# Two-layer attention and expert kernel on one core: group buffers, scatter order, unused norm products, and one tile step moved

## What is computed

```python
x = x + L0_attn(xn) + L0_ffn(xn);  xn = layernorm(x)
x = x + L1_attn(xn) + L1_ffn(xn)
# L0_attn: q, k(2), v(2) = xn + xn @ W.T + b; feature map silu(.)+0.5 on q and k, divided by
#          the norm of each head (16 heads of 8); state = prod over the 2 kinds of k^T v;
#          out = q state; layernorm with gain and bias; @ Wo.T + bo
# L0_ffn:  8 experts of 128x128, the best one for each token, y * its softmax weight
# L1_attn: 16 heads, window of 32, plus 8 latent heads over 64 pooled rows, gates, @ w_out
# L1_ffn:  8 experts 128 -> 512 (relu) -> 128, the best two for each token, weighted sum
```

## Time and profile before

| | |
|---|---|
| three runs | 658.37, 658.41, 660.02 us |
| profiled execution | 655.52 us; its span 653.8 us |
| busy in the span | PE 510.1 (78%), DVE 410.6 (63%), ACT 280.7 (43%), POOL 272.4 us (42%) |
| chain that ended last | PE 50%, DVE 20%, no visible wait ("issue") 10%, POOL 9%, ACT 6%, DMA 3% |
| mean granted TensorE clock | 0.859 of full speed |

### The profile page before, as it was taken

How to read it: one execution, slowest core, us unless ns; L and a number is a source line. 1 busy time by engine, 2 the same in 40 slices (tenths; PEclk the granted TensorE clock), 3 DMA queues, 4 the chain that set the end, 5 groups by cost and what they waited for, 6 DMA issues and landing times.

```text
span 653.8 us, 19837 instructions
## 1 busy us (share of the span) xinstructions
PE 510.1 (78%) x7216; PEld 419.8 (64%) x7216; DVE 410.6 (63%) x1113; ACT 280.7 (43%) x714; POOL 272.4 (42%) x321
## 2 busy tenths in 40 slices
PE   6929947696642786389778889998999898988765
PEld 3926737585630573267556878896889687977544
DVE  6678867575536946995968364646465554565572
ACT  1315742443320115153536666565656564654320
POOL 6064573455758000277676223141314140414830
PEclk8658967987885757598999999999999998999775
DMA  9999113434402600011112634242415240510991
GB/s 246 220 249 190 37 50 93 135 113 140 140 18 69 188 1 2 17 55 53 47 56 61 218 110 151 69 162 86 155 57 183 77 158 35 180 63 14 135 209 48
DMA packets 80237, 70.12 MB, mean 107 GB/s; under 512 B 7604, under 2 KB 65779, under 8 KB 80142
## 3 DMA queue, kind: packets, MB, share of 16 engines
q1 hardware_dynamic: 62528, 50.87, 28.1%
q0 software_dynamic: 15072, 16.90, 11.3%
q10 hardware_dynamic: 2542, 1.08, 0.7%
HBM read 22.73 MB, written 23.22 MB: 70 GB/s over the span
## 4 chain that ended last, share of the span: by engine, by line
PE 50%; DVE 20%; issue 10%; POOL 9%; ACT 6%; DMA 3%; DVEq 0%; ACTq 0%; POOLq 0%; SPq 0%
PE psum L1816 8%; PE psum L1805 8%; POOL sorted L694 6%; PE psum L1304 3%; PE psum L559 2%; PE psum L852 2%; PE psum L1238 2%; DVE st_all L498 2%; PE psum L974 2%; PE psum L1349 2%; DVE x_all L490 2%; ACT arena L1440 2%; PE psum L1327 2%; PE psum L1359 2%; PE psum L953 2%
## 5 line engine op out<-in xcount | busy, mean ns | idle before, releaser
L1878 POOL DMA_INDIRECT ydram<-xnT_all,f_id x71 | 69.3, 976 | 177.1 <-DVE f_id L1851 124.2
L694 POOL DMA_INDIRECT sorted<-xr_all,slot x96 | 95.7, 997 | 44.6 <-issue 26.5
L1836 ACT ACTIVATE xr_all<-psum,b1T 128x128 f32<-128x128 f32 x284 | 81.1, 369 | 28.9 <-PE psum L1805 27.8
L1816 PE MATMUL psum<-w,xr_all 128*128 x568 | 76.6, 278 | 1.6 <-DVE xnT_all L1859 1.4
L1805 PE MATMUL psum<-xr_all 128*128 128x128 f32 x568 | 77.1, 279 | 0.0
L1859 DVE TENSOR_TENSOR xnT_all<-psum,b_bc 128x128 f32<-128x128 f32 x71 | 20.7, 292 | 88.2 <-PE psum L1816 84.6
L1805 PEld LDWEIGHTS psum<-xr_all 128*128 128x128 f32 x568 | 69.8, 194 | 4.0 <-issue 3.4
L1816 PEld LDWEIGHTS psum<-w,xr_all 128*128 128x128 f32 x568 | 69.2, 192 | 3.2 <-issue 2.6
L1507 ACT ACTIVATE arena<-arena 128x512 f32<-128x512 f32 x32 | 20.1, 630 | 67.0 <-DVE arena L1594 65.5
L837 POOL DMA_INDIRECT ydram<-arena,g_id x40 | 40.6, 1015 | 11.2 <-issue 10.7
L1327 PE MATMUL psum<-arena 128*128 128x128 f32 (+3 forms) x64 | 22.5, 471 | 17.6 <-DVE arena L1574 10.4
(11 more groups left out here) (284 smaller groups left out, 1166.6 us busy)
## 6 DMA issues: line engine op xcount, KB each, us to landing
xr_all<-arena SPq DMA_DIRECT2D x71, 256.0 KB
arena<-mix SPq DMA_DIRECT2D x40, 128.0 KB, 2.0
sorted<-pre_row SPq DMA_DIRECT2D x1, 4680.0 KB, 29.4
xnT_all<-sorted SPq DMA_DIRECT2D x18, 260.0 KB, 3.2
x_all<-ydram POOLq DMA_DIRECT2D x16, 256.0 KB, 9.7
sorted<-pre_row SPq DMA_DIRECT2D x1, 2600.0 KB, 21.1
arena<-sorted SPq DMA_DIRECT2D x10, 260.0 KB, 3.0
x_all<-in_L_attn_x_dram SPq DMA_DIRECT2D x8, 256.0 KB, 6.0
```

The costliest lines, as they stand in the source:

```text
L694: g.indirect_dma_start(out=dst, out_offset=bass.IndirectOffsetOnAxis(ap=slot[:, choice, t:t + 1], axis=0), in_=xr_all[:, t, :], in_offset= ...
L1816: mm = pe.matmul(psum[:, 3, 0:C], f_hT[n % 3][:, j * P:(j + 1) * P], w2[:, bass.ds(e * FC + j, 1), :].rearrange("p a f -> p (a f)"), start ...
L1836: ins = act.activation(f_hT[n % 3][:, j * P:(j + 1) * P], psum[:, 1 + rr % 2, j * P:(j + 1) * P], ACT.Relu, bias=b1T[:, bass.ds(e * FC + j ...
L1878: g.indirect_dma_start(out=ydram, out_offset=bass.IndirectOffsetOnAxis(ap=f_id[rr][:, 1:2], axis=0), in_=f_y[rr % 4], in_offset=None, boun ...
```

## The change

- `norm_pe`, both layers: in front of each batch's wait for its rows, TensorE makes 5 products of 128x256 bf16 whose result nobody reads (PSUM bank 2, columns 256 to 511).
- `biases_pool`: the 10 instructions run first on the 384 columns of the query and key biases, with no wait for VectorE, and later, after VectorE's fifth step, on the 128 columns of the output bias. TensorE waits for the second set only before `states`, VectorE before its features.
- Layer 0, TensorE: queries and keys of batch 0 come before `routing_pe`. ScalarE's two tanh of batch 0 stand alone, in the same place of its order as before.
- `states`: `g_y` and `g_id` have four buffers, `g_y` in the space of the transposed rows (`xnT`) of batches 0 to 3; VectorE waits for the scatters of group n-4 instead of n-2. POOL scatters `mid` in front of the addition.
- `mixed` on ScalarE: one of the three tile steps stands between the copy of the queries and that of the keys.

```diff
+        def unused_halves(pe, n):
+            for _ in range(n):
+                pe.matmul(psum[:, 2, 256:512], onesb[:, 0:P], onesb[:, 0:256], start=True, stop=True,
+                          skip_group_check=True)
...
+        def bias_parts(g, lo, hi, done):
+            q = slice(lo, hi)
+            g.tensor_copy(bparts[:, 0, q], brow[:, q]).then_inc(s_bp, 1)
...
         def biases_pool(g):
             g.wait_ge(s_w, 16 * N_W)
+            bias_parts(g, 0, 3 * C, 0)
             g.wait_ge(s_setv, N_SETV)
...
+            bias_parts(g, 3 * C, 4 * C, N_BP)
...
+        def two_deep(eng, stage, begun=False):
+            if not begun:
+                stage(eng, None, (0, 0))
...
                     k = b + B * layer
+                    unused_halves(pe, 5)
                     pe.wait_ge(s_xn, k + 1)
...
-        g_y = [view(4 * C).rearrange("p (j c) -> p j c", j=4) for _ in range(2)]
+        GY, GID = 4, 4
+        g_y = [xnT(b).rearrange("p (j c) -> p j c", j=4) for b in range(GY)]
+        g_id = [view(4, dt=I32) for _ in range(GID)]
...
+        def group_scattered(eng, n):
+            if n >= 0:
+                eng.wait_ge(g_sc[n % GID], (n // GID + 1) * 64)
...
         def group_numbers(v, n):
-            if n >= 2:
-                v.wait_ge(g_sc[r], n // 2 * 64)
+            group_scattered(v, n - GID)
...
         def group_results(v, n):
-            if n >= 2:
-                v.wait_ge(g_sc[r], n // 2 * 64)
+            group_scattered(v, n - GY)
...
+        def feat_tanh(act, cur):
...
         def feat_act(act, prev, cur):
-            if cur:
+            if cur and prev:
+                feat_tanh(act, cur)
...
         def state_pool(g, three, two, one, mid, behind):
+            group_pool(g, mid)
             if three:
...
-            group_pool(g, mid)
             group_pool(g, behind)
...
         def y0_loads(sp):
-            for r in range(2):
-                sp.wait_ge(g_sc[r], 64 * (NGR // 2))
+            for n in range(NGR - GID, NGR):
+                group_scattered(sp, n)
...
                 queries(b + 1)
+                tiles.go(1)
                 keys(b + 1)
                 pooled_rows(b + 1)
-                tiles.go(3)
+                tiles.go(2)
...
             routing_act(act, 0)
+            feat_tanh(act, (0, 0))
             two_deep(act, feat_act)
...
             routing_dve(v, 0)
+            v.wait_ge(s_bp, 2 * N_BP)
             two_deep(v, feat_dve)
...
-            routing_pe(pe, 0)
             pe.wait_ge(s_bp, N_BP)
             pe.wait_ge(s_lgu, 1)
-            two_deep(pe, feat_pe)
+            feat_pe(pe, None, (0, 0))
+            routing_pe(pe, 0)
+            two_deep(pe, feat_pe, True)
             pe.wait_ge(s_w2, 16 * N_W2)
+            pe.wait_ge(s_bp, 2 * N_BP)
```

More of the change, by code:

```diff
@@ L412, in build @@
         N_SETV = 5
+        def bias_parts(g, lo, hi, done):
+            q = slice(lo, hi)
+            g.tensor_copy(bparts[:, 0, q], brow[:, q]).then_inc(s_bp, 1)
+            g.wait_ge(s_bp, done + 1)
+            g.tensor_tensor(bres[:, q], brow[:, q], bparts[:, 0, q], ALU.subtract).then_inc(s_bp, 1)
+            g.wait_ge(s_bp, done + 2)
+            g.tensor_copy(bparts[:, 1, q], bres[:, q]).then_inc(s_bp, 1)
+            g.wait_ge(s_bp, done + 3)
+            g.tensor_tensor(bres[:, q], bres[:, q], bparts[:, 1, q], ALU.subtract).then_inc(s_bp, 1)
+            g.wait_ge(s_bp, done + 4)
+            g.tensor_copy(bparts[:, 2, q], bres[:, q]).then_inc(s_bp, 1)
+            g.wait_ge(s_bp, done + 5)
+            for k in range(3):
+                g.tensor_scalar(bparts[:, k, q], bparts[:, k, q], ident[0:3, k:k + 1], None, ALU.mult).then_inc(s_bp, 1)
+            g.wait_ge(s_bp, done + 8)
+            g.tensor_tensor(bparts[:, 0, q], bparts[:, 0, q], bparts[:, 1, q], ALU.add).then_inc(s_bp, 1)
+            g.wait_ge(s_bp, done + 9)
+            g.tensor_tensor(b3[0:3, q], bparts[:, 0, q], bparts[:, 2, q], ALU.add).then_inc(s_bp, 1)
+        N_BP = 10
         def biases_pool(g):
             g.wait_ge(s_w, 16 * N_W)
+            bias_parts(g, 0, 3 * C, 0)
             g.wait_ge(s_setv, N_SETV)
[L418 to L435, removed]
+            bias_parts(g, 3 * C, 4 * C, N_BP)
         def layer1_dve(v):
@@ L746, in build @@
         g_ld = [sem(f"g_ld{r}") for r in range(2)]
-        g_id = [sb(f"g_id{r}", [P, 4], I32) for r in range(2)]
         g_idr = sem("g_idr")
         g_wl = [sem(f"g_wl{r}") for r in range(2)]
-        g_sc = [sem(f"g_sc{r}") for r in range(2)]
+        g_sc = [sem(f"g_sc{r}") for r in range(GID)]
         NGR = NT0 // 4
@@ L832, in group_pool @@
             n -= 1
-            r = n % 2
             g.wait_ge(g_idr, n + 1)
@@ L837, in group_pool @@
                 g.indirect_dma_start(out=ydram, out_offset=bass.IndirectOffsetOnAxis(
-                    ap=g_id[r][:, j:j + 1], axis=0), in_=g_y[r][:, j, :], in_offset=None,
-                    bounds_check=ydram.shape[0] - 1, oob_is_err=False).then_inc(g_sc[r], 16)
+                    ap=g_id[n % GID][:, j:j + 1], axis=0), in_=g_y[n % GY][:, j, :], in_offset=None,
+                    bounds_check=ydram.shape[0] - 1, oob_is_err=False).then_inc(g_sc[n % GID], 16)
         def feat_pe(pe, prev, cur):
@@ L864, in keys_psum @@
             return psum[:, 2 + 2 * r:4 + 2 * r, :].rearrange("p a c -> p (a c)")
-        def feat_act(act, prev, cur):
-            if cur:
-                b, r = batch(cur), cur[0] % 2
-                act.wait_ge(a_q, b + 1)
-                act.wait_ge(a_zqr, b + 1)
-                act.activation(a_uq[r], psum[:, r, :], ACT.Tanh, scale=0.5).then_inc(a_tqr, 1)
-                act.wait_ge(a_k, b + 1)
-                act.wait_ge(a_ukr, b + 1)
-                act.activation(a_tk[r], keys_psum(r), ACT.Tanh, scale=0.5).then_inc(a_tkr, 1)
+        def feat_tanh(act, cur):
+            b, r = batch(cur), cur[0] % 2
+            act.wait_ge(a_q, b + 1)
+            act.wait_ge(a_zqr, b + 1)
+            act.activation(a_uq[r], psum[:, r, :], ACT.Tanh, scale=0.5).then_inc(a_tqr, 1)
+            act.wait_ge(a_k, b + 1)
+            act.wait_ge(a_ukr, b + 1)
+            act.activation(a_tk[r], keys_psum(r), ACT.Tanh, scale=0.5).then_inc(a_tkr, 1)
+        def feat_act(act, prev, cur):
+            if cur and prev:
+                feat_tanh(act, cur)
             if prev:
@@ L1181, in attn1_init @@
             g.wait_ge(s_phase, 3)
-            for r in range(2):
-                g.wait_ge(g_sc[r], 64 * (NGR // 2))
+            for n in range(NGR - GID, NGR):
+                group_scattered(g, n)
             step = S // NL
```

7 lines of the change are left out of this document (2 added, 5 removed).

## The result

The changed kernel takes 630.8 us, the median of four runs (628.40 to 636.65), against 658.39 us of the kernel before: ratio 0.9605, 95% interval 0.9518 to 0.9692. Forecast were 630.4 us within 621 to 643. The profiled execution took 628.40 us (span 626.7) against 655.52 (span 653.8). The sum comes out near; its terms do not all.

The account below looks back on a forecast made before the run. Each stage was taken to have its own limit, with PE busy 78%. Terms of -15.5, -5.4, -1.0 and -6.1 summed to -28.0 us: 627.5 profiled, 630.4 for the median, 8-in-10 range 621 to 643.

Parts of the forecast that it names:

- States, 15.5 us: States stage: four buffers and scatters ahead of POOL's addition save 15.5 us, with ends of 9.9 and 19.3.
- 19.3 us by POOL's side: States stage: 40 scatters and 6 additions take POOL 58.3 us from the first result at 119.7, allowing 19.3 us.
- TensorE's 16.4: States stage by TensorE's side: 9.9 us of idle time, 5.3 of clock and 1.2 of last addition, together 16.4 us.
- step of 5.3 us for the clock: States stage: without the idle time TensorE's clock holds in three places, 3 x (4.00 - 2.24) = 5.3 us.
- Halves in layer 0, 2.8 us: Layer 0's norm: the five unused products a batch keep TensorE at 2.4 GHz and save 2.8 us.
- at the high level: Layer 0's norm at 2.4 GHz: 2.5, 0.75 and 0.4 us gained, about 0.9 lost; low level would cost 4.2 us.
- second rival: Norm of layer 0: POOL's biases hold VectorE, TensorE idles before batch 4, its clock falls; total 634.7 us, chance 0.12.
- Layer 1's norm, -1.0 us: Layer 1's norm: TensorE enters the last four batches at the low clock, recovers midway; saves 1.0 us.
- Routing, 2.6 us: Layer 0's routing: without POOL's bias work beside it VectorE's routing gets 2.6 us shorter, ends 0.9 and 3.8.
- the head start: Layer 0: TensorE has batches 0 and 1 done before VectorE's features; taken as nothing, ends -1.9 and +1.5 us.
- they end about when the mask is ready: Layer 0: moved queries and keys end some 5 us after the logits, so they don't delay the routing products.
- Tile step, 6.1 us: Mixed batches: ScalarE's copy no longer stands behind the keys, four TensorE waits go; saves 6.1 us, ends 6.4 and 3.

Follow-up runs that it names:

- set 2: Second set of later runs, undisturbed: kernel before (656.5 us), states change alone, addition back in front of the scatters, two buffers; the last three 641.2, 636.4 and 641.6 us.
- e8: Changed kernel with filled norm, routing products first and all ten bias instructions in one piece beside the routing: 723.4 us, ratio 0.9908 to the kernel before, disturbed set.
- filled kernel: Changed kernel with 33 instead of 5 unused products before batches 2 and 4 of layer 1's norm: 724.0 us, ratio 0.9882 to the kernel before.
- kernel with the states alone: Kernel before with only four buffers, their indices in the arena and scatters ahead of the addition: 641.2 us, ratio 0.9760 to the kernel before.
- set 1: First set of later runs, disturbed (kernel before 732.1 us): changed kernel, unused products in layer 0 only, none, filled: 731.6, 728.4, 732.5, 724.0 us.
- set 3: Third set, other chip, disturbed (kernel before 730.0 us): filled norm, then with tile step undone, routing products first, biases also back: 722.65, 730.5, 718.5, 723.4 us.

## Why the prediction was right, and where it wasn't

*States, 15.5 us:* right in cause, and near in size. From the first scatter the stage gave 15.6 us; set 2 shows that the buffers carry it. But the forecast's 19.3 us by POOL's side counts from the first result at 119.7, and so does the fair comparison: 17.5 us, between TensorE's 16.4 and POOL's 19.3. The step of 5.3 us for the clock held in two places of three.

*Halves in layer 0, 2.8 us:* the step "at the high level" was right; the logits gained 1.9. Missing was the price of the biases beside it, which I had set to 0: 0.3 us by the changed kernel's own logits against those of e8 (35.06 and 34.74), up to 1.2 by another trace. Even without that price the gain is 2.2 us, so some 0.6 us of the 2.8 are unexplained. The second rival was half true: VectorE's rows for batches 4 and 5 begin at 25.13 instead of 22.48 us, 2.7 us late where I had 1.4 or more, but TensorE's wait was only 0.60 us, and the clock held.

*Layer 1's norm, -1.0 us:* wrong. The step that failed is "I expect it to recover only midway". It didn't recover at all, and 1.05 us of products a batch were added to a slow stage: 3.0 us lost instead of 1.0 gained. The premise was misread too. TensorE stood idle not "before batches 4 and 5" but before batches 2 and 4, as these rows of the kernel before show, so six batches and not four came at the low level:

```profile
222.85 1.11 PE L553 MATMUL psum<-ident,xr_all 128*128 128x128 f32 x4 [3.67 <-DVE xr_all L522]
...
230.71 1.12 PE L553 MATMUL psum<-ident,xr_all 128*128 128x128 f32 x4 [2.78 <-DVE xr_all L522]
```

The filled kernel shows the idle time as the cause.

*Routing, 2.6 us:* 2.3 measured, but it is a difference of two: the biases give 3.7, where I had taken 2.6, and the head start, set to nothing within -1.9 to +1.5, cost 1.3 us or more in the traces that ran it at the low clock and nothing in the two that did not. The failed step is "they end about when the mask is ready": in the first trace queries and keys of batch 0 ran at 0.61 and 0.54 and the routing products began at 40.6 us, with the mask ready at 38.7. At 1.00 the step holds (39.0 and 38.8). That the two misses nearly cancel is luck.

*Tile step, 6.1 us:* 6.8 in the two traces, 5.3 to 7.4 over all undisturbed ones. The step that said that nothing else waits was incomplete: 3.5 us of waits vanish net, as waits for L1879 came in. TensorE's busy time in the stretch fell too, from 216.75 to 214.62 us. What else makes up the whole is not settled, and so is how much of it the tile step alone is worth on an undisturbed chip: the one run that undoes it alone is disturbed.

*Not in the sum at all:* layer 1's attention, 3.6 us longer, and the end, 6.1 us shorter. In the attention the same 2138 or so products kept TensorE busy 86.7 us before and 92.1 after, at a mean granted clock of 0.85 and 0.81. Over the six undisturbed traces the length follows that clock: 119.2, 120.2 and 120.4 us at 0.85, 121.4 at 0.83, 122.7 at 0.81, 124.6 at 0.80. So the loss goes with the clock; what in the change lowers it is open, and a share may be chance. The last of POOL's scatters of sorted rows ends 5.5 us before the first tile product before and 8.5 us after, so POOL's scatters don't account for the longer stage. For the end, the windows of before and after at the same work (stretch, length, busy PE, PEld, DVE, ACT, POOL; clock; DMA; GB/s):

```profile
614.00:624.00 10.00, 9.32 (x220) 6.94 (x220) 5.74 (x12) 2.31 (x6) 10.00 (x11) 0.70 1.41 175
```

```profile
593.00:603.00 10.00, 7.97 (x221) 5.68 (x220) 8.41 (x15) 2.25 (x6) 10.00 (x12) 1.00 1.35 167
```

Nearly the same 220 products take 9.32 us of TensorE at 0.70 and 7.97 at 1.00; over the whole end it is busy 42.6 us before and 38.1 after. In front of the first window lies a stall in which the engine waited for nothing that the profile shows:

```profile
612.09 0.66 PE L1231 MATMUL psum<-wgv,cmp_ 128*128 128x64 f32 x5 [2.81 <-issue]
```

After, that stall isn't there; two shorter ones stand elsewhere (1.36 and 1.25 us). As the kernel with the states alone has the old end (60.6 us, 0.68 in its window) and the three with changed products on TensorE have 53.6, 55.3 and 58.2, I take it that the place of such a stall moved with TensorE's instructions. That is argued, not shown: no run moved it alone, and in the disturbed sets kernels with the same products have ends of 56.0 to 63.5 us, so the 6.1 us may be chance in part.

So the total is right because two unforeseen losses, 4.0 us (layer 1's norm) and 3.6 us, stood against an unforeseen gain of 6.1 us and some 0.7 us of small differences. The terms for buffers and tile step were sound; that 27.1 us came of 28.0 forecast is luck for the rest.

Of what was run, only the filled norm is better than the changed kernel beyond the noise: 724.0 against 731.6 us in set 1. With the routing products first besides, set 3 has 718.5 against 722.7 us, which the intervals don't separate (730.0 us is the kernel before there). What either takes on an undisturbed chip was not measured.

## What to carry to other kernels

Unused products that were to hold TensorE's clock had to fill its idle time here: beside a wait of 4 us that they left open they only lengthened the stage, so try them in front of the batches whose input comes late, as many as the wait is long. A buffer that comes free with a landing DMA deserves more copies before the order of a queue is touched: here 14.5 us against 7.6, and 17.5 together. Choose the marks of a stage so that the edit can't move one of them: "first scatter" hid 1.9 us of the order. And where two edits meet on one engine's rows (biases and norm, batch 0 and routing products), price each alone, and in more than one trace: one gain of 2.3 us was 3.7 less 1.3, and the 1.3 came and went with the clock.

## What the runs showed of the hardware

In the disturbed sets (1 and 3) TensorE nearly stood while POOL issued a row of scatters. First the changed kernel in set 1, attention of layer 1; then the same work undisturbed:

```profile
288.22 1.09 PE L1323 MATMUL psum<-arena,mix 32*32 32x256 f32 x5 [0.36 <-issue]
288.75 0.97 POOL L708 DMA_INDIRECT sorted<-xr_all,slot  x1 [0.30 <-issue]
289.65 1.08 PE L1323 MATMUL psum<-arena,mix 32*32 32x256 f32 x4 [0.34 <-issue]
290.03 0.97 POOL L708 DMA_INDIRECT sorted<-xr_all,slot  x1 [0.30 <-issue]
...
297.02 0.55 ACT L1537 ACTIVATE arena<-psum 128x128 f32<-128x128 f32 x2 [13.88 <-remote]
```

```profile
257.37 2.54 PE L1323 MATMUL psum<-arena,mix 32*32 32x256 f32 x64
258.14 0.97 POOL L708 DMA_INDIRECT sorted<-xr_all,slot  x1 [0.30 <-issue]
```

POOL's scatters take 0.97 us in both. TensorE gets 4 to 5 products started every 1.43 us in the one and 64 in 2.54 us in the other, and ScalarE waits 13.88 us, until 2.2 us after a row of twelve scatters has ended. The states stage takes 83.3 to 84.2 us in all eight such traces, against 60.5 to 62.9 undisturbed with four buffers. The two norm stages are unchanged (35.1 and 46.85 us for the changed kernel), and so is the routing at either clock. The Trainium skill ("SBUF — State Buffer", section "Who interferes with whom") states that TensorE and ScalarE never wait for another engine's use of SBUF. The undisturbed rows agree (64 products in 2.54 us beside a scatter); the disturbed ones show "issue", a wait in front of the engine, so that they don't contradict it, and they don't show the cause of that wait. The changed kernel loses all its gain there (0.9976). What disturbs the chips (it was seen on two, and one of them ran undisturbed in set 2), why the gain is lost, and whether the kernel before suffers in the same places, isn't known: of before there is no trace from such a set.
